# Feed-forward stage with the rounding step of h in PSUM, one gate bank, and a reordered drain

## What is computed

```python
x = x + mamba(layernorm(x))          # 4 layers, x is 8 x 256 x 128, float32
x = x + ffn(layernorm(x))
x = x + attention(layernorm(x))      # 16 heads, position bias, causal
x = x + ffn(layernorm(x))

def ffn(x):                          # H, I = 128, 352
    gate = fp4_linear(x, w_gate); y = fp4_linear(x, w_up)
    return fp4_linear(silu(gate) * y, w_down)

def fp4_linear(x, w):                # both operands rounded to a grid of 8 magnitudes, by blocks of 16
    return fp4_quant_dequant(x) @ fp4_quant_dequant(w).T
```

## Time and profile before

| | us |
|---|---|
| median of 3 runs | 1041.48 (1040.91 to 1042.05) |
| the profiled execution's own time | 1041.14 |
| its span, first to last instruction | 1039.4 |
| DVE busy / PE busy / ACT busy / POOL busy | 902.7 / 950.2 / 761.0 / 760.1 |
| first feed-forward, from the first product of h to the end of the last down | 740.6 to 802.0 |
| second feed-forward, likewise, to the last addition | 980.0 to 1037.1 |
| granted TensorE clock, mean of the span | 0.969 of full speed |

### The profile page before, as it was taken

How to read it: one execution, slowest core, us unless ns; L and a number is a source line. 1 busy time by engine, 2 the same in 40 slices (tenths; PEclk the granted TensorE clock), 3 DMA queues, 4 the chain that set the end, 5 groups by cost and what they waited for, 6 DMA issues and landing times. The chain is left out here.

```text
span 1039.4 us, 29750 instructions
## 1 busy us (share of the span) xinstructions
PE 950.2 (91%) x11909; PEld 577.4 (56%) x11909; DVE 902.7 (87%) x1724; ACT 761.0 (73%) x1683; POOL 760.1 (73%) x426
## 2 busy tenths in 40 slices
PE   5799999999999999999999999987477899999775
PEld 2455555555555555555555565655256566666445
DVE  6889998999989999899998999998799657787597
ACT  5888898898988989889898898885333245555442
POOL 1688999989999999899998999997353323333243
PEclk9799999999999999999999999999798889999899
DMA  6845443544444444545445454430760110000001
GB/s 191 279 128 166 153 156 125 166 145 182 147 149 152 148 151 145 183 145 160 143 133 169 140 166 143 141 129 2 161 141 1 21 22 12 13 2 2 2 0 41
DMA packets 69272, 120.88 MB, mean 116 GB/s; under 512 B 40072, under 2 KB 51152, under 8 KB 60112
## 3 DMA queue, kind: packets, MB, share of 16 engines
q1 hardware_dynamic: 69136, 118.98, 36.3%
HBM read 111.10 MB, written 6.29 MB: 113 GB/s over the span
## 5 line engine op out<-in xcount | busy, mean ns | idle before, releaser
L902 DVE TENSOR_TENSOR_SCAN hid<-decay,acc 128x256 f32<-128x256 f32 x1024 | 604.6, 664 | 40.9 <-PE acc L539 40.5
L1002 POOL TENSOR_TENSOR prod<-hid,c_rep 128x1024 f32<-128x1024 f32 x256 | 600.1, 2373 | 44.3 <-DVE hid L902 33.3
L765 ACT ACTIVATE decay<-delta,a_neg 128x255 f32<-128x255 f32 x1024 | 428.2, 501 | 47.7 <-DVE hid L902 47.5
L539 PE MATMUL acc<-b_diag,du_t 64*64 64x256 f32 x4096 | 273.2, 383 | 15.9 <-DVE hid L902 12.2
L567 PE MATMUL ring<-prod,ident 64*64 64x256 f32 x4096 | 255.5, 379 | 2.2 <-POOL prod L1002 2.2
L539 PEld LDWEIGHTS acc<-b_diag,du_t 64*64 64x64 f32 x4096 | 147.8, 134 | 124.8 <-DVE hid L902 55.4
L567 PEld LDWEIGHTS ring<-prod,ident 64*64 64x64 f32 x4096 | 152.0, 133 | 83.5 <-issue 22.9
L1915 POOL TENSOR_SCALAR_AFFINE_SELECT att_probs<-att_probs 128x512 f32<-128x512 f32 x64 | 40.9, 639 | 109.3 <-ACT att_probs L1958 106.9
L1958 ACT ACTIVATE att_probs<-acc 128x384 f32<-128x384 f32 x128 | 55.8, 488 | 55.8 <-PE acc L1732 55.8
L444 PE MATMUL ring<-xpad,diag_cw 64*64 64x512 f32 x512 | 60.6, 590 | 0.0
L1116 POOL TENSOR_TENSOR ffn_h_value<-ffn_h,ffn_h_inv 128x704 f32<-128x704 f32 x16 | 23.7, 1479 | 43.5 <-DVE ffn_h_value L1139 32.5
(11 more groups left out here) (180 smaller groups left out, 1259.5 us busy)
## 6 DMA issues: line engine op xcount, KB each, us to landing
c_rep<-c_rows SPq DMA_DIRECT2D x64, 1024.0 KB, 4.8
b_diag<-diag_rows SPq DMA_DIRECT2D x62, 512.0 KB, 3.8
diag_rows<-zeros SPq DMA_DIRECT2D x2, 2048.0 KB, 12.4
att_qk<-in_pos_q SPq DMA_DIRECT2D x4, 768.0 KB
att_qk<-in_pos_k SPq DMA_DIRECT2D x4, 768.0 KB
att_qk<-att_dense SPq DMA_DIRECT2D x24, 64.0 KB
resid<-in_x SPq DMA_DIRECT2D x4, 256.0 KB, 3.2
c_rows<-bc SPq DMA_DIRECT2D x64, 8.0 KB, 1.5
```

The lines of the kernel that those rows point to most:

```text
L539: last = nc.tensor.matmul(inj[m * HALF:(m + 1) * HALF, K % 2, at:at + HALF * SG], du_t[rows, n % 2, e, chans:chans + HALF], b_diag[rows, K ...
L765: last = nc.scalar.activation(decay[:, K % DECAYS, s, 1:], delta[:, n % 2, h, e * SEQ + 1:(e + 1) * SEQ], ACT.Exp, scale=a_neg[:, lay(n) % ...
L902: last = nc.vector.tensor_tensor_scan(hid[:, K % HIDS, s, :], decay[:, K % DECAYS, s, :], rows[:, s, :], 0.0, ALU.mult, ALU.add)
L1002: nc.gpsimd.tensor_tensor(prod[:, K // 2 % PRODS, h], hid[:, K % HIDS, :, :], c_rep[:, g, :, at], ALU.mult).then_inc(s_prod, 1)
```

## The change

The step of h is one buffer in PSUM (`held`, acc 2 and 192 columns of acc 3): ACT writes it there, DVE's two rounding instructions read it there, and `scalar_step(c)` waits until `round(c-1)` is over. The exponent bits still go to SBUF. To make room, gate has one bank (ring 1), up has ring 2 and acc 0, the first two thirds of the turned h share ring 0 with x, the last third is in acc 1, and down has one bank (ring 3). So `gate_up` waits in tile n for Silu of n - 1; `turn_h(k)` waits for the last `copy_x` that could still need ring 0; `down(k)` waits for `add(k-1)`.

The orders are new. DVE in turn k: `exponent(k-1)`, `add(k-4)`, `hidden(k)`, `round(k-1)`. POOL: waits for the exponent of k-1, then `dequant(k-2)`, `normal(k)`. PE: `gate_up(k+1)`, `turn_x`, `turn_h(k-2)`, `down(k-3)`. ACT: `step(k-1)`, `gate(k+1)`, `copy_x`, `copy_h(k-2)`. In ffn2 ACT normalises x chunk 3 behind the first step's Silu, and DVE makes its offset behind `hidden(0)`. In ffn1 the attention's first normalisation stands ahead of the last round, and all four strips stand ahead of the barrier.

```diff
-    def __init__(self, core, sb, tag, blocks, depth=2):
+    def __init__(self, core, sb, tag, blocks, depth=2, held=None):
...
+    def steps(self, i):
+        return self.step[:, i, :] if self.held is None else self.held
     def scalar_step(self, a, c):
         a.wait_ge(self.s_exponent, c + 1)
-        self.core.nc.scalar.activation(self.step[:, i, :], self.step[:, i, :], ACT.Relu, ...
+        if self.held is not None and c:
+            self.s_round.wait(a, "rounded", c - 1)
+        self.core.nc.scalar.activation(self.steps(i), self.step[:, i, :], ACT.Relu, ...
...
-        gate_bank = [bank(ring, 1), bank(ring, 2)]
-        up_bank = [bank(ring, 3), bank(acc, 0)]
-        hT_bank = [bank(acc, 1)[:, 0:2 * P], bank(acc, 1)[:, 2 * P:4 * P], bank(acc, 2)[:, 0:2 * P]]
-        down_bank = [bank(acc, 3)[:, 0:2 * P], bank(ring, 0)[:, 0:2 * P]]
+        qh = Rounder(core, sb, "h", HCOLS // BLK, 4, acc[:, 2 * BANK:2 * BANK + HCOLS])
+        x_bank, gate_bank, up_bank = bank(ring, 0), bank(ring, 1), [bank(ring, 2), bank(acc, 0)]
+        hT_bank = [bank(ring, 0)[:, 0:2 * P], bank(ring, 0)[:, 2 * P:4 * P], bank(acc, 1)[:, 0:2 * P]]
+        down_bank = bank(ring, 3)[:, 0:2 * P]
... vector
+                for k in range(HSTEPS + 1):
+                    if 1 <= k:
+                        qh.vector_exponent(v, k - 1)
+                    if k in (1, 3) and k // 2 + 2 >= early:
+                        x.q.vector_exponent(v, k // 2 + 2)
+                    if k >= 4:
+                        add(k - 4)
+                    if attention and k == HSTEPS - 1:
+                        v.wait_ge(s_add, 2)
+                        attention.norm.vector_moments(v, 0)
                     if k < HSTEPS:
                         hidden(k)
+                    if k == 0 and early:
+                        norm.vector_offset(v, 3)
+                    if k == 1:
                         x.vector_scales(v, 3)
+                    if attention and k == HSTEPS:
+                        attention.norm.vector_normalise(v, 0)
+                    if 1 <= k:
+                        qh.vector_round(v, k - 1)
...
                 if attention:
+                    attention.wait(v)
+                    attention.vector_strips(v, 0)
                     attention.norm.vector_normalise(v, 1)
+                    for g in range(1, HGROUPS):
                         attention.vector_strips(v, g)
... gpsimd
+                for k in range(HSTEPS + 2):
+                    if k >= 2:
+                        p.wait_ge(qh.s_exponent, min(k, HSTEPS))
+                        h_dequant(k - 2)
+                    if k < HSTEPS:
+                        h_normal(k)
... tensor: gate_up, turn_h, down and the loop
-                        need(t, s_silu, n - 1)
+                        need(t, s_silu, n)
+                    t.wait_ge(s_xTc, 3 if k < 2 else 4)
-                    need(t, s_add, k - 1)
+                    need(t, s_add, k)
-                for k in range(HSTEPS + 3):
+                for k in range(HSTEPS + 2):
                     if k + 1 < HSTEPS:
                         gate_up(k + 1)
+                    if k >= 2:
+                        turn_h(k - 2)
                     if k >= 3:
-                        turn_h(k - 3)
-                    if k >= 4:
-                        down(k - 4)
+                        down(k - 3)
... scalar
                 if early:
                     copy_x(0)
                     norm.scalar_rstd(a, 3)
-                    norm.scalar_normalise(a, 3)
                     nc.scalar.preload_act_table_set(SILU)
...
                 gate(0)
                 copy_x(1)
+                if early:
+                    norm.scalar_normalise(a, 3)
```

More of the change, by code:

```diff
@@ L1134, in vector_round @@
         nc, i = self.core.nc, c % self.depth
-        value, step = self.value[:, i, :], self.step[:, i, :]
+        value, step = self.value[:, i, :], self.steps(i)
         v.wait_ge(self.s_step, c + 1)
@@ L1316, in _ @@
                     attention.norm.vector_moments(v, 1)
-                for k in range(HSTEPS - 2, HSTEPS):
+                for k in range(HSTEPS - 3, HSTEPS):
                     add(k)
                 if attention:
+                    attention.wait(v)
+                    attention.vector_strips(v, 0)
                     attention.norm.vector_normalise(v, 1)
-                    attention.wait(v)
-                    for g in range(2):
+                    for g in range(1, HGROUPS):
                         attention.vector_strips(v, g)
@@ L1332, in h_dequant @@
                     qh.pool_dequant(p, qh.blocked(hq[:, k % 2, :]), k)
-                if early:
-                    x.pool_normal(p, 3)
-                else:
+                if not early:
                     x.pool_normal(p, 0)
@@ L1358, in turn_x @@
                     need(t, s_xTc, c)
+                    need(t, s_hTc, 2 if c == 3 else 0)
                     for i in range(CH_TILES):
-                        last = nc.tensor.transpose(ring[:, i * P:(i + 1) * P], x.xq[:, c, i * P:(i + 1) * P], ident[:, :])
+                        last = nc.tensor.transpose(x_bank[:, i * P:(i + 1) * P], x.xq[:, c, i * P:(i + 1) * P], ident[:, :])
                     last.then_inc(s_xT, 1)
@@ L1411, in _ @@
                     attention.wait(t)
-                    t.wait_ge(s_silu, 2 * HSTEPS)
-                    t.wait_ge(s_xTc, CHUNKS)
+                    t.wait_ge(s_hTc, HSTEPS)
+                    qh.s_round.wait(t, "rounded", HSTEPS - 1)
                     attention.tensor_strips(t, 0)
                     t.wait_ge(s_add, HSTEPS)
-                    attention.tensor_strips(t, 1)
+                    for g in range(1, HGROUPS):
+                        attention.tensor_strips(t, g)
             @block.scalar
@@ L1434, in copy_h @@
                     need(a, s_down, k - 1)
-                    nc.scalar.activation(hqT[:, k % 2, 0:2, :], bank(acc, 1).rearrange("p (j n) -> p j n", j=2), ACT.Copy)
+                    nc.scalar.activation(hqT[:, k % 2, 0:2, :], bank(ring, 0).rearrange("p (j n) -> p j n", j=2), ACT.Copy)
                     nc.scalar.activation(hqT[0:FK[2], k % 2, 2, :], hT_bank[2][0:FK[2], :], ACT.Copy).then_inc(s_hTc, 1)
@@ L1799, in project_out @@
                     banks.fill(last, "proj", b)
-                for g in range(2, HGROUPS):
-                    tiles.tensor_strips(t, g)
                 project_v(0)
```

74 lines of the change are left out of this document (23 added, 51 removed).

## The result

The changed kernel takes 1066.51 us (median of 4 runs, 1064.17 to 1067.58), the kernel before in the same runs 1041.2: ratio 1.025, 95% interval 1.0228 to 1.0272. It is slower, as forecast, but by 25 us where 9 were forecast, and outside the range.

| stretch | before | after | difference | forecast |
|---|---|---|---|---|
| up to the first product of h | 740.6 | 739.3 | -1.3 | 0 |
| ffn1, first product to last down | 61.4 | 67.2 | +5.8 | +3.5 |
| last down to the attention's first scores | 9.6 | 10.5 | +0.9 | +0.9 |
| attention, first scores to ffn2's first transpose | 162.4 | 174.3 | +11.9 | 0 |
| ffn2, to the last addition | 63.1 | 70.2 | +7.1 | +4.7 |

What follows compares the result with a forecast made beforehand. DVE set the pace, held up by POOL; after the change a 5.86 us round trip through PE would rule. First feed-forward with strips +4.4, second +4.7, sum 9.1 on 1041.14: 1050.2, with 0.34 for the median 1050.5; range 1042 to 1056.

Steps and rivals of the forecast that it cites:

- The frame: Whole kernel: Mamba stage and inside of the attention untouched, only the two feed-forwards and the attention's entry can move.
- The strips: Entry of the attention: all four strips behind the last down, mask casts no longer hidden, scores at +10.5 against 9.6, +0.9.
- Low clock in the loops: Feed-forwards: PE near 1.2 GHz in ffn1's drain (1.5 us), for a gate product in ffn2's head, and in ffn2's drain.
- The rival with a costless clock: Both feed-forwards: round trip holds, PE keeps 2.4 GHz, ACT's step comes in time; 1044.2, range 1042 to 1046, chance 0.20.
- third rival: Rounds in the loops: PSUM doesn't free DVE from POOL, step 6.6, about +14, 1064; chance 0.04.
- The waits up to `hidden(7)` of ffn1: Loop of ffn1: DVE waits 10.2 us beside 39.5 of work, so `hidden(7)` starts 49.6 behind the first product, +7.2.
- The head of ffn2: Start of ffn2: first Silu 1.0 earlier, normalisation ahead of the second step's; waits 11.1 up to `hidden(7)`, which starts +8.9.
- an idle time of DVE near 3 in step 1: Sign for the profile, second feed-forward: DVE idle near 3 us in step 1, ended by Silu.
- The round trip: Settled loop steps: DVE's addition waits for its chain through PE, 5.86 us a step, and 7.15 once per stage.
- The drains: From `hidden(7)` to the stage's end: 15.3 us in ffn1, 14.9 in ffn2, against about 19 before.
- PSUM frees DVE from POOL: Rounding in the loops: with the step in PSUM POOL doesn't hold DVE; instruction 0.88, 0.51 per step and three drain stalls removed.
- The gate bank: Round trip in the loops: with one gate bank, Silu to the second tile's gate product adds 0.58 us.

Runs made afterwards that it cites:

- e17: Changed kernel plus unused matmuls in both feed-forwards' early pauses and ahead of the barrier, addition behind next h, old head of ffn2: 1038.5 us, ratio 0.9983.
- e12: Kernel before, with two unused matmuls of 512 columns on PE ahead of the attention's barrier: 1042.7 us, ratio 1.0027.

## Why the prediction was wrong

- *The frame failed first.* "The inside of the attention [is] untouched by the diff, so only the two feed-forwards and the entry of the attention can move." It took 11.9 of the 24.4 us, which is what its 28.5 us more of low clock cost at 0.42 each. The strips were costed by their work (+0.9, and the scores came at +10.49 where +10.5 was said), not by what PE's new pause at the barrier does to the clock of the stage behind. The row was there: in the earlier trace rows PE stands 1.79 at the barrier, and the two strips of products behind it, which lay between this pause and the scores, were what the change took away.
- *Low clock in the loops was the term that was too small.* The forecast gave it 1.5 in one drain and some in the head of ffn2; filling the pauses took 4.0 and 3.1 out of the stages, more than the 2.3 and 2.4 that were missing (+5.8 against +3.5, +7.1 against +4.7). The rival with a costless clock was further off still. The figure of the third rival, 1064, is the nearest of all to the 1066.5, by luck: it comes from rounds held up by POOL, and L1145 stayed at 886 ns.
- *The waits up to `hidden(7)` of ffn1:* 10.2 were said, of them 8.9 without those for POOL beside the small scales; of this kind were measured 2.75, 1.50, 1.94, 1.13, 1.95, 0.54, 0.54, sum 10.4, against 1.7, 1.6, 1.1, 1.1, 2.0, 0.7, 0.7. That is 1.5 of the 1.8 by which the loop is longer than forecast (51.4 against 49.6). The two that were missed by about 1 us are those with PE at 1.2 GHz ahead (granted clock 0.50 from 739 to 743, and from 755 on):

```profile
742.57 0.52 DVE L1275 TENSOR_TENSOR ffn_h<-ffn_silu,acc 128x352 f32<-128x352 f32 x1 [2.75 <-ACT ffn_silu L1434]
765.66 0.89 DVE L1143 SCALAR_TENSOR_TENSOR ffn_h_value<-acc,ffn_h_value 128x704 f32<-128x704 f32 x1 [1.94 <-ACT acc L1136]
```

- *The head of ffn2:* 11.1 of waits were said and 12.0 measured (2.75, 1.43, 0.17, 1.48, 0.99, 1.27, 0.91, 1.94, 0.54, 0.54), in a loop of 50.3 where 47.9 was said. The sign "an idle time of DVE near 3 in step 1 [...], ended by Silu" failed: such a wait, 2.75, stands in step 0, and the one of step 1 was 1.48. The first Silu came 1.0 sooner, as said.
- *The round trip was right:* 5.80 and 5.81 against 5.86, 7.21 against 7.15, ended by the down product as said; so was what decides it, since with the addition behind `hidden` the step is 5.17 against the 5.18 said for DVE alone. The drains were right (15.8 and 14.9 against 15.3 and 14.9), with one miss inside: the attention's normalisation, counted at 1.03, took 2.07 while POOL's dequantisation ran (795.71, 1.39). The new order puts them side by side.

```profile
795.87 2.07 DVE L1057 TENSOR_SCALAR normed<-resid,meanvar,rstd 128x128 f32<-128x128 f32 x4
```

- *PSUM frees DVE from POOL:* right, 886 ns where SBUF gives 1955; worth 0.45 us in each settled step, and 5.9 us over both stages by one profile of each. That this would be lost without the sooner rounding (+44 us with the old orders) was nowhere in the text.
- *The gate bank* was given a hand-over on the round trip; measured were 1.6 and 3.1 us, at the head. What it costs on the round trip of the settled steps was not measured.

What stays open: why the same pause is followed by low clock in one execution and not in another, whether the attention's own pause of 1.11 us causes the low stretch behind it, and whether the 1.8 us by which e17 is faster than the kernel before are more than scatter.

## What to carry to other kernels

Before moving work off an engine's idle place, ask what the clock of TensorE behind that place is worth: here a pause of 1.65 us that cost nothing in its own stage was followed by some 10 us at half speed in the next. When an addition that reuses a single bank stands ahead of the next step's work, the whole chain through PE becomes the period; putting it one place later gave DVE's own pace back. Judge such a change stage by stage and over several executions, as the twelve of one kernel (e12) lay between 1035.7 and 1050.9. And look in the trace whether an added instruction ran where it was meant to.

## What the runs showed of the hardware

- In the attention's small products (17 rows) TensorE stayed at 1.2 GHz for 8 and for 20 us on end (820 to 828, 836 to 856), with PE busy 4.00 of 4.00 us in each window looked at. Each us of low clock cost the attention 0.42 us. The Trainium skill (TensorE: Matmul & The Clock Gate, "HAM oscillation — how this bites in real kernels") tells of waits for data between groups of products, longer ones than here, each of which drops the clock. The runs agree in kind, and showed it behind a pause of 1.65 us in some of the variants that have it; with two unused matmuls in the pause it didn't fall there in any of five.
- A ScalarE write of the step to PSUM took 0.85 us, to SBUF 0.88, and DVE's first rounding instruction with an operand in PSUM 883 ns against 884: PSUM cost nothing here.
- DVE's tensor-scalar normalisation, one SBUF input and scalars by pointer, took nearly twice its time while GpSimd's dequantisation ran (2.07 against 1.11).
